# Four tiles of 32 columns in place of one of 128 for some TensorE products of a macaron transformer layer

## The reference

```python
Wq1, Wq2 = quantize(W1), quantize(W2)        # each weight becomes -1, 0 or 1
def ffn(x): return relu(x @ Wq1.T + b1) @ Wq2.T + b2      # 128 -> 512 -> 128
x = x + 0.5 * ffn(LN(x))
x = x + attention(LN(x))                      # 16 heads of 8 channels
x = x + 0.5 * ffn(LN(x))
# attention: q, k, v = x @ W.T + b; rope(q), rope(k);
# softmax(q k^T / sqrt(8)) v per head; then @ Wo.T + bo
```

## Time and profile before

| | us |
|---|---|
| median of 3 runs | 526.37 |
| lowest, highest | 526.09, 526.54 |
| the profiled execution | 526.69 |
| its span | 524.9 |
| TensorE matmul busy | 494.7 |
| VectorE busy | 410.9 |
| ScalarE busy | 347.9 |
| GpSimd busy | 203.8 |

### The profile page before, as it was taken

The page is one execution under the profiler, slowest core; times in us unless marked ns, Lnnn a source line. Parts: engine busy times, 40 slices in busy tenths (PEclk is TensorE's granted clock), DMA queues, the critical chain, the costliest instruction groups (busy, mean ns, idle before and its releaser), DMA issues.

```text
span 524.9 us, 8681 instructions
## 1 busy us (share of the span) xinstructions
PE 494.7 (94%) x3211; PEld 233.2 (44%) x3211; DVE 410.9 (78%) x644; ACT 347.9 (66%) x429; POOL 203.8 (39%) x226
## 2 busy tenths in 40 slices
PE   6688899899999999999999999998999899999996
PEld 3456425253454435353445443533353344443445
DVE  5777987859897699877887699778977997898124
ACT  5617665657767586767867668675776677578741
POOL 3407173708155281907261383153333650005002
PEclk8899999999999999999999999998999999999999
DMA  8056047003350246004540256032602351000000
GB/s 277 20 180 147 21 160 186 2 3 121 128 118 1 61 164 161 3 22 124 158 86 2 61 186 139 19 115 92 159 7 62 145 144 38 22 2 3 2 20 21
DMA packets 19990, 44.35 MB, mean 84 GB/s; under 512 B 2860, under 2 KB 5420, under 8 KB 18924
## 3 DMA queue, kind: packets, MB, share of 16 engines
q1 hardware_dynamic: 18636, 41.96, 28.1%
q10 hardware_dynamic: 1312, 1.84, 1.1%
HBM read 20.58 MB, written 18.87 MB: 75 GB/s over the span
## 4 chain that ended last, share of the span: by engine, by line
PE 74%; DVE 15%; ACT 3%; issue 3%; DMA 2%; POOL 1%; ACTq 0%; DVEq 0%; POOLq 0%
PE heads_acc L576 21%; PE unit L559 14%; PE unit L540 12%; PE side L638 10%; DVE maxima L900 8%; PE side L632 4%; PE side L618 3%; PE side L626 2%; PE side L614 2%; ACT probs L782 2%; ACT hidden L772 1%; PE side L604 1%; PE heads_acc L646 1%; PE side L599 1%; DMA q_scratch<-q_parts 1%
## 5 line engine op out<-in xcount | busy, mean ns | idle before, releaser
L900 DVE TENSOR_REDUCE maxima<-unit 128x2 f32<-128x1024 f32 x256 | 305.0, 1219 | 63.2 <-PE unit L540 62.5
L782 ACT ACTIVATE probs<-unit 128x1024 f32<-128x1024 f32 x256 | 256.4, 1025 | 106.8 <-PE unit L559 106.4
L576 PE MATMUL heads_acc<-probs,v_heads 128*32 128x512 f32 x1024 | 136.4, 608 | 0.5 <-ACT probs L782 0.4
L559 PE MATMUL unit<-q_stack,k_stack 64*128 64x512 f32 x512 | 118.3, 461 | 8.5 <-DVE maxima L900 7.6
L540 PE MATMUL unit<-k_stack,q_stack 62*128 62x512 f32 x512 | 114.2, 443 | 2.9 <-DMA q_stack<-q_scratch 1.2
L559 PEld LDWEIGHTS unit<-q_stack,k_stack 64*128 64x128 f32 x512 | 47.8, 184 | 69.6 <-DVE maxima L900 31.7
L540 PEld LDWEIGHTS unit<-k_stack,q_stack 62*128 62x128 f32 x512 | 48.4, 185 | 60.7 <-ACT probs L782 27.9
L638 PE MATMUL side<-w_q,hidden 128*128 128x128 f32 x416 | 56.8, 285 | 0.0
L638 PEld LDWEIGHTS side<-w_q,hidden 128*128 128x128 f32 x416 | 49.4, 191 | 13.4 <-issue 9.3
L385 POOL TENSOR_TENSOR rope_a_k<-k,cos_t 128x512 f32<-128x512 f32 x7 | 8.9, 1275 | 102.8 <-ACT k L769 102.8
L1056 POOL TENSOR_SCALAR var_eps_ffn<-mean_var_ffn 128x4 f32<-128x4 f32 x15 | 3.7, 248 | 114.4 <-DVE mean_var_ffn L871 114.4
(11 more groups left out here) (144 smaller groups left out, 465.1 us busy)
## 6 DMA issues: line engine op xcount, KB each, us to landing
k_scratch<-k_parts SPq DMA_DIRECT2D x16, 512.0 KB, 2.9
q_scratch<-q_parts SPq DMA_DIRECT2D x14, 512.0 KB, 2.9
k_stack<-k_scratch SPq DMA_DIRECT2D x16, 384.0 KB, 6.0
q_stack<-q_scratch SPq DMA_DIRECT2D x16, 384.0 KB, 7.2
resid<-in_x SPq DMA_DIRECT2D x8, 256.0 KB, 4.5
k_stack<-k_scratch SPq DMA_DIRECT2D x16, 128.0 KB, 2.7
k_swap<-k SPq DMA_DIRECT2D x14, 128.0 KB, 2.3
q_swap<-q SPq DMA_DIRECT2D x14, 128.0 KB, 2.3
```

The source lines that it names most:

```text
L559: mm = pe.matmul(to[:, e, :], k_stack[part, quad // NQ % 2, pair, kt * P:(kt + 1) * P], q_stack[part, quad // NQ % 2, pair, :], start=True ...
L576: mm = pe.matmul(heads_acc[32 * j:32 * j + 32, :], v_heads[:, b % 2, at, ODD * odd:ODD * odd + 32], probs[:, burst % RING, j, :], start=(k ...
L782: act.activation(probs[:, burst % RING, 2 * pp:2 * pp + 2, :], unit_of(PLACE["exp", n]), ACT.Exp, scale=SCALE).then_inc(s_exp, 1)
L900: dve.tensor_reduce(maxima[:, quad % 2, :, r], unit_of(PLACE["max", k]), AX_X, ALU.max).then_inc(s_max, 1)
```

## The change

A helper `column_tiles` splits a product of 128 columns of weights into four of 32 columns. Each writes its quarter of the partitions of the same PSUM bank, and reads the same moving operand. The `up`s in the prologue and in the lists use it, and so do the q and k projections of batches 1 to 7. Of an `up`, the four tiles of `x_hi` come first, then the four of `x_lo`. The semaphore is raised by the last tile.

```diff
+TILE_COLS = 32
...
+            def column_tiles(to, lhs, rhs, start, stop):
+
+                for c in range(0, P, TILE_COLS):
+                    mm = pe.matmul(to[c:c + TILE_COLS, :], lhs[:, c:c + TILE_COLS], rhs, start=start, stop=stop)
+                return mm
+
...
                 elif name in ("q", "k"):
                     pe.wait_ge(s_xT, index + 1)
-                    pe.matmul(to, w_proj[:, "qk".index(name), :], x_T[:], start=True, stop=True).then_inc(s_qk_psum[name], 1)
+                    column_tiles(to, w_proj[:, "qk".index(name), :], x_T[:], True, True).then_inc(s_qk_psum[name], 1)
...
                     for n, part in enumerate((x_hi, x_lo)):
-                        mm = pe.matmul(to, w1_q[:, arg * P:(arg + 1) * P], part[:], start=(n == 0), stop=(n == 1))
+                        mm = column_tiles(to, w1_q[:, arg * P:(arg + 1) * P], part[:], n == 0, n == 1)
                     mm.then_inc(s_up[which], 1)
```

## The result

| | before | after |
|---|---|---|
| median, us | 526.45 (526.09 to 528.16, 4 runs) | 522.73 (521.03 to 523.04, 4 runs) |
| ratio | | 0.9907, 95% interval 0.9878 to 0.9935 |
| profiled execution, its span | 526.69, 524.9 | 522.56, 520.8 |

The account below looks back on a forecast made before the run. TensorE's own list was taken as the bound, wholly from 183 to 299 us. It shortens by 4.55 us, of which 3.0 plus 0.6 count: 526.69 - 3.6 = 523.1, 0.3 lower as median: 522.8 us; range 521.2 to 525.9.

Parts of the forecast that it names:

- A lone up: An up standing between score products in the lists: splitting it costs 0.03 us more, 48 x 0.03 = +1.4 us (0 to +1.9).
- A join of up and burst: 28 places in the lists where an up adjoins a burst of values: the shape change goes, 0.13 us each, -3.6 us.
- the 0.21 of split and join: q and k projections: 14 splits at -0.06 us each (-0.8) and 11 joins with bursts at 0.15 each (-1.65).
- the first half of B: Rival: a drain between float16 and float32 tiles of one shape stays, so -3.6 falls away, 525.6 us; B's chance 0.08.
- the second half of B: Rival: the ups' tiled float16 weight loads get slow, 188 in place of 96 ns, +4.3 us, 526.1 us; held to be 0.03.
- C: Rival: instruction supply to TensorE becomes the bound; 536 us at 106 ns a pair, slower from 82 ns; chance 0.07.
- D: Rival: tiles of one moving operand don't run side by side; an up takes 1.8 us, +58 us, some 585; chance 0.03.
- 90% of -3.35 = -3.0: From 125 to 299 us: TensorE's list shortens by 3.35 us, of which 90% counts in the time.
- half of -1.2 = -0.6: Outside 125 to 299 us: TensorE's list shortens by 1.2 us, half of which counts, since VectorE shares the chain from 299.
- rival A: The gain in the middle is mostly handed to VectorE and ScalarE, leaving -1.5, 524.9 us; chance 0.13.
- the sign of being wrong: VectorE's maxima turning up in the chain of 183 to 299 us would show the forecast wrong.
- E's stretches: Rival: half-clock stretches after TensorE waits, up to 1.7 us each; two more give 526.2, one less 521.1; chance 0.05 (two more).

## Why the prediction was right, and where it was not

**Prices of single steps.** Right in the main, where nothing else is waited for. A lone up costs 0.01 more, not 0.03. A join of up and burst gives 0.10 behind the up and, where a score product follows, 0.04 in the burst (0.96 from 195.81 to the next start), 0.14 for 0.13. A projection in tiles takes 0.88 where the burst follows and 1.05 was before, 0.17 for the 0.21 of split and join. Float16 beside float32 tiles of one shape does not drain, so the first half of B is out. The tiles' float16 load takes

```profile
L584 PEld LDWEIGHTS side<-x_hi,w_q 128*32 128x32 f16 x196 | 5.1, 93 | 19.1 <-ACT hidden L779 10.9 <-issue 4.2 <-DVE attn_out L924 1.7
```

93 ns, against 96 for 128 columns. The rule on Fast Weight Load that the Trainium skill has in TensorEngine Tiling (Array Packing), section Restrictions, shows no cost at this size, and the second half of B is out. C is out by 28 ns a pair, D by the four starts of a pass inside 0.03 us and 0.55 us an up.

**What counts.** This is the step that failed: "I count 90% of -3.35 = -3.0". It measured 1.3 between the kernels shown, and 1.3 and 1.4 between the two pairs that differ in the tiles alone. "Outside I count half of -1.2 = -0.6" measured 0.8 and 0.85. So rival A, to which I gave 0.13, holds for the middle: the gain is handed to another engine, above all to ScalarE. The chain from 180 to 237 us is no longer one of TensorE lines alone; the maxima, which I had named as the sign of being wrong, are not in it, but two lines of ScalarE are:

```profile
by line: PE heads_acc L577 23.5%; PE unit L560 19.0%; PE unit L541 16.4%; PE side L645 14.2%; PE side L584 8.6%; PE side L633 3.8%; ACT hidden L779 3.5%; PE side L621 3.2%; ACT probs L789 3.2%; PE side L611 2.2%; PE side L606 1.6%; PE side 
```

The gain is taken back at the next place that waits for another engine. In the trace after such places are seen in the weight loads:

```profile
187.60 0.19 PEld L560 LDWEIGHTS unit<-q_stack,k_stack 64*128 64x128 f32 x2 [0.41 <-DVE maxima L907]
...
197.24 0.19 PEld L560 LDWEIGHTS unit<-q_stack,k_stack 64*128 64x128 f32 x2 [0.28 <-DVE maxima L907]
...
225.32 0.42 PEld L621 LDWEIGHTS side<-ident_f,normed_attn 128*128 128x128 f32 x4 [0.97 <-ACT hidden L779]
236.57 0.16 PEld L584 LDWEIGHTS side<-x_T,w_proj 128*32 128x32 f32 x8 [0.86 <-ACT k L776]
```

The first two wait for a unit from VectorE; the gain of one join was given back between 196.77 and 197.24, 0.47 us where 0.33 was before. The third waits until ScalarE has read the up out of the side bank. There the burst and its follower stood so before, and so after:

```profile
224.58 1.06 PE L576 MATMUL heads_acc<-probs,v_heads 128*32 128x512 f32 x8
225.58 0.66 PE L614 MATMUL side<-ident_f,normed_attn 128*128 128x128 f32 x4
```

```profile
224.23 1.03 PE L577 MATMUL heads_acc<-probs,v_heads 128*32 128x512 f32 x8
225.32 0.66 PE L621 MATMUL side<-ident_f,normed_attn 128*128 128x128 f32 x4
```

From the burst's start to the next it is 1.09 instead of 1.00, so the 0.09 won in front of the burst is lost behind it. This is the commonest loss: of the 20 ups in front of a burst, six have a transpose into the side bank behind the burst (1.00 before, 1.09 after) and three another up (1.00 before, 1.01 after, where an up behind a burst otherwise starts at 0.88). All nine are in the middle. The last of the weight loads above is q behind the burst in k, burst, q, burst: the bank is k's until ScalarE has copied it, so this join gives nothing (0.99 from burst to q after, 1.00 before).

My reading erred in the view. I took "matmuls cover 115.98 of 116.00 us" and a chain of TensorE lines alone as proof that nothing else bounds TensorE. A score product's record lasts 0.39 to 0.50 us while the next may start after 0.23, so a wait of up to 0.2 us leaves no gap in the matmul row. The waits of the weight loads had it, before the change, from 183 to 299 us:

```profile
PEld unit L540 <- ACT probs L782: 4.1, 11, 0.8
PEld unit L559 <- DVE maxima L900: 3.7, 10, 0.8
```

The range has a slip too: with nothing lost and a lone up at no cost, its low end would be 526.37 - 4.55 - 1.4 = 520.4, not 521.2. It didn't matter for 522.73.

**What made the number come out.** 3.6 were forecast and 2.1 to 2.2 came so. The profiled execution gained 2.2 more by the phase of the split (1.1 at 355, 1.1 at 411), and about as much by the clock inside the lists as it lost to it behind them, 1.4 against 1.7. E's stretches were seen to come and to go, but their net was small here. Whether the one at the end belongs to the tiles is open: four of the six profiles with all these products whole and in tiles of 32 columns have it, near 506 to 511 us, and none of the other eight. The range held for a reason that the working did not contain; that 522.73 met 522.8 is luck.

## What to carry to other kernels

Price a step by the distance of starts, and ask what it is worth by the waits of the weight loads: here a matmul row without gaps did not say that TensorE was the bound. Where products of one shape stand beside others, giving them the neighbour's tile shape saved the change of shape, 0.1 us each, where the order stayed and the next product did not wait for the bank that was just filled. And before a gain of a few us is put down to an edit, look whether small VectorE ops on SBUF stand beside GpSimd products, and try to hold GpSimd back by a wait there: a shift of 0.1 us decided over 1.1 us, twice.

## What the runs showed that I had not expected

A VectorE split of 16 numbers took 0.17 us alone and up to 1.3 beside a GpSimd product; starting 0.02 us behind that product or 0.06 ahead of it decided. Pairs of load and matmul of 32 columns were supplied at 28 ns. In the one profile without the lower parts, the prologue with fewer products took 4.1 us more: the clock was granted at 0.51 between 8 and 18 us instead of 0.83.
